# Routing of an expert layer moved four tiles at a time into the end of the attention before it

## The chip, the cores and the metric

One core of a Trainium2 chip. The metric is the device time of one execution in microseconds (us). A core has TensorE (PE, with its weight loads shown as PEld), VectorE (DVE), ScalarE (ACT), GpSimd (POOL) and SyncE (SP), each with its own queue that is worked off in order; they meet only at semaphores. Transfers are issued by SP, ACT and POOL and run on 16 shared DMA engines.

## The reference

A decoder layer on x of 8 x 256 tokens with 256 features, in float32, in three residual parts:

```python
x = x + fast_weight_attention(layernorm(x), W_qkvb, W_o, ln_g, ln_b)
x = x + cross_attention(layernorm(x), context, Wq, Wk, Wv, Wout, bout)   # 8 heads of 128
x = x + experts(layernorm(x), router_w, w1, w2)                          # 8 experts, 1024 hidden

def experts(x):
    probs = softmax(x @ router_w)              # [2048, 8]
    idx = argmax(probs); gate = probs[idx]
    pos = running count of earlier tokens of the same expert
    keep = pos < 256
    expert_in[idx, pos] = x                    # 8 experts x 256 places
    y = (gelu(expert_in @ w1) @ w2)[idx, pos] * gate * keep
```

## The kernel before

Tokens lie in 16 tiles of 128 (HALVES = 2 halves of the 256 rows times T = 8 steps). Tile s * 8 + t holds half s of step t. FLAT lists the tiles in the order of the tokens (t = 0: halves 0 and 1, then t = 1, ...), which is the order in which the router must count.

Three blocks run one after another, each ended by a barrier of all engines: `fast_weight_block`, `cross_block`, `expert_block`.

`cross_block` projects queries, keys and values, then runs one loop over SLOTS = 128 query tiles (8 heads x 16 tiles). In step s of each engine's loop: TensorE computes the scores of tile s (`scores`, L1254), ScalarE the exponential (L1382), VectorE the maxima (L1120, L1122) and a 32x32 transpose (L1135). Since only 32x32 blocks are turned there, 16 moves by DMA (`move`, L939, half issued by SP, half by ACT) finish each transposition for one fourth of the keys of a group of four tiles. LAG = 7 steps behind the scores the moved blocks are split into a high part (ACT, L1376) and a low part (POOL, L1045, and on the last units DVE, L1168), and TensorE adds the weighted values (`weighted`, L1271). Every four units, ACT copies the sum out (`copy_oT`, L1401), TensorE multiplies by the output weights in two halves (`out_project`, L1283), and VectorE scales and adds it to `hall` (`add_output`, L1152). In the last head VectorE then takes the statistics of the two tiles (`row_stats`, L1159 and L1161). After step 127 there are no more scores: steps 128 to 137 are the drain, with only the last weighted sums and outputs. A head's tiles are taken in the order of their number, so the first eight are half 0 of all steps.

`expert_block` begins after the barrier with the routing of all tiles: DVE and ACT normalise the rows (L1625 to L1631), ACT copies the residual rows (L1735), then four "quads" of four tiles in FLAT order go through `row_transposes` (L1791), `copy_zt`, `row_logits` (L1800), `choose` (L1660 to L1673, maximum, one-hot, running counts), `positions` (L1807, L1808) and `place` (L1681 to L1690, slot numbers as int32). POOL scatters each tile's rows into `expert_in` in DRAM by an indirect DMA (L1595), in order, and behind the 16 scatters splits off the low parts of w1 of two experts (L1579). ACT makes the high parts (L1749, L1753), DVE the low part of w2 (L1622). When all scatters have landed, SP loads expert 0's rows (L1550), TensorE transposes them (L1823) and multiplies (L1834, L1846). Eight experts follow each other in a pipeline of two buffers.

```python
            for n, m in enumerate(FLAT):
                if n % 4 == 0:
                    pool.wait_ge(slot_ready, n // 4 + 1)
                pool.indirect_dma_start(xe, ..., z[:, m], None, ...).then_inc(scattered, 16)
            split_low(0, 0)
            split_low(1, 1)
            pool.wait_ge(scattered, 16 * TILES)
```

Of the kernel before, what the change touches and what calls it, by code (L numbers as in the profile page):

```python
# [34 lines left out]
HI, LO = 0, 1  # L35

# [37 lines left out]
WST, CTX = 0, 4 * 4 * 1024  # L74


def fast_weight_block(nc, x, w_qkvb, w_o, context, w_k, w_v, wst, cnat, ident, hall, stats, xe, dots_d, wts_d, beta_d):
# [13 lines left out]
    with ExitStack() as ctx:  # L91
# [12 lines left out]
        for name, span in (("wv", 4 * 2 * DC * NH * DH), ("dots", 4 * 2 * HALVES * T * 2 * HN * CELL),  # L104
                           ("wtok", 4 * TILES * NH * T), ("wqk", 4 * 2 * DC * NH * 2 * DH),
                           ("F", 4 * 2 * BLKS * (2 * BLK + 2)), ("hT", 4 * 2 * DC * TOK), ("ebuf", 4 * 2 * 2 * CHUNK),
                           ("DR", 4 * HG * BLKS * HN * CELL), ("tmp", 4 * 2 * 7 * GCOL)):
            at[name] = start + size
            size += (span + 31) // 32 * 32
# [21 lines left out]
        wo = sb("fw_wo", [P, INNER // P, D])  # L131
# [612 lines left out]
def cross_block(nc, x, ln_g, ln_b, bout, w_q, w_out, wst, cnat, ident, hall, stats, qd, kd, vd):  # L744
# [13 lines left out]
    with ExitStack() as ctx:  # L758
# [9 lines left out]
        for name, span in (("kT0", 4 * 2 * TOK), ("moved", 4 * 3 * TOK), ("kT1", 4 * 2 * TOK), ("pT", 4 * 4 * TOK),  # L768
# [20 lines left out]
        mx = sb("xa_mx", [P, 2])  # L789
        nb = sb("xa_nb", [P, 2])  # L790
        rs = stats
        rinv = sb("xa_rinv", [P, TILES])
        bn = sb("xa_bn", [P, 6])

        OUTS = 5
# [24 lines left out]
        PJ = len(pj)  # L820

# [30 lines left out]
        rows_ln = sem("xa_ln")  # L852

# [30 lines left out]
        def among(s):  # L884
# [3 lines left out]
            return range(EARLY + sum(AMONG[:s]), EARLY + sum(AMONG[:s + 1]))  # L888

# [67 lines left out]
        def _(sp):  # L957
# [31 lines left out]
            for p in range(SLOTS):  # L989
# [10 lines left out]
                for d in (0, 1):  # L1000
                    for a in (0, 2, 1, 3):
                        move(sp, p, a, a ^ d)

        @block.gpsimd
        def _(pool):
# [44 lines left out]
            for s in range(SLOTS):  # L1050
# [4 lines left out]
                for c in chunks_of(s):  # L1055
                    chunk_low(c)

        @block.vector
        def _(dve):
# [79 lines left out]
            def add_output(g, k):  # L1139
# [11 lines left out]
                for m in range(2):  # L1151
                    last = dve.scalar_tensor_tensor(hall[:, i + m], Y[k][:, m], rinv[:, i + m:i + m + 1],  # L1152
                                                    hall[:, i + m], ALU.mult, ALU.add)
                last.then_inc(y_used, 1)

            def row_stats(g, k):
                dve.wait_ge(y_used, 2 * g + k + 1)
                for m in (g % 4 * GT + 2 * k, g % 4 * GT + 2 * k + 1):
                    dve.bn_stats(bn[:], hall[:, m]).then_inc(rows_ln, 1)  # L1159
# [11 lines left out]
            for s in range(SLOTS + LAG + 3):  # L1171
# [5 lines left out]
                if p >= GT and p % GT < 2:  # L1177
# [6 lines left out]
                elif s - LAG + 1 < SLOTS:  # L1184
                    for r in (0, 1):
                        low_part(2 * (s - LAG + 1) + r)

        @block.tensor
        def _(pe):
            def transposes(n):  # L1190
                if n == CTX_BANKS:
                    pe.wait_ge(z_ready[0], 1)
                if n == CTX_BANKS + Z_BANKS // 4:
                    pe.wait_ge(z_ready[1], 1)
                if n >= 4:
                    pe.wait_ge(tp_lo, n - 3)
                for k in range(4):
# [3 lines left out]
                    else:  # L1201
                        c, m = (n - CTX_BANKS) // (TILES // 4), (n - CTX_BANKS) % (TILES // 4) * 4 + k
                        src = z[:, m, c * P:(c + 1) * P]
# [82 lines left out]
            for s in range(SLOTS + LAG + 2):  # L1286
# [7 lines left out]
                if p >= GT and p % GT < 2:  # L1294
                    out_project(p // GT - 1, p % GT)

        @block.scalar
        def _(act):
# [104 lines left out]

            for n in range(Q0, Q0 + 8):
                copy_out(n)
# [7 lines left out]
            for s in range(SLOTS + LAG + 1):  # L1413
                p = s - LAG
                if p >= GT and p % GT == 0:
# [23 lines left out]
def expert_block(nc, r_w, w1, w2, out, ident, hall, stats, xe):  # L1439

    with ExitStack() as ctx:
# [10 lines left out]
        FLAT = [s * T + t for t in range(T) for s in range(HALVES)]  # L1454
        QUADS = TILES // 4
        z = sb("ex_z", [P, TILES, ROW])
        rw = sb("ex_rw", [P, DC, E])
        lg = sb("ex_lg", [P, TILES, E])
        ex = sb("ex_ex", [P, TILES, E])
        oh = sb("ex_oh", [P, TILES, E])  # L1460
        pre = sb("ex_pre", [P, TILES, E])
        rank = sb("ex_rank", [P, E])
        mx = sb("ex_mx", [P, TILES])
        top = sb("ex_top", [P, TILES])
        gate = sb("ex_gate", [P, TILES])
        token = sb("ex_token", [P, TILES], I32)
        pos = sb("ex_pos", [P, TILES])
        slot = sb("ex_slot", [P, TILES])
        sloti = sb("ex_sloti", [P, TILES], I32)
# [425 lines left out]
```

## Time and profile before

| | us |
|---|---|
| median of 3 runs | 1476.18 (1470.36 to 1476.22) |
| profiled execution | 1479.12 |
| its span | 1477.3 |

| engine | busy us | share of the span |
|---|---|---|
| PE | 1344.4 | 91% |
| PEld | 1102.6 | 75% |
| DVE | 1132.8 | 77% |
| ACT | 935.0 | 63% |
| POOL | 867.6 | 59% |

The profile is of one execution. Times in it are counted from the start of the span. A row of the timeline is: start, duration, engine, line of the kernel, operation, output<-inputs, shapes, number of instructions merged into the row, and in brackets the idle time before it with what ended it. "ACTq" and "SPq" are DMA issues by those queues. TensorE's granted clock is given as a share of 2.4 GHz: 1.00 is 2.4 GHz, 0.50 is 1.2 GHz. A busy TensorE is not one at its peak, since the ends of its matmuls are modelled.

### The profile page before, as it was taken

The numbers are of one execution on the slowest core, as the hardware profiler recorded it, in microseconds if no ns is written. First come the engines' busy times: TensorE is split into PE (matmuls) and PEld (weight loads), VectorE is DVE, ScalarE is ACT, GpSimd is POOL, SyncE is SP. The second block draws the span as 40 slices with busy tenths as digits, with TensorE's granted clock in tenths as the row PEclk, the third lists the DMA queues.
The fourth block names the chain that finished last, engine by engine and source line by source line (L and its number), as shares of the span: only waits on it lengthen the run. The fifth ranks groups of instructions, "written<-read, shape, count | busy, mean of one in ns | idle before, by whom it ended". The sixth has DMA issues, their size and how long they took to land. (4 is left out here: it accounts for less than half of the span.)

```text
span 1477.3 us, 22028 instructions
## 1 busy us (share of the span) xinstructions
PE 1344.4 (91%) x7240; PEld 1102.6 (75%) x7240; DVE 1132.8 (77%) x1726; ACT 935.0 (63%) x1278; POOL 867.6 (59%) x525
## 2 busy tenths in 40 slices
PE   3999999998999799999999999999999999765897
PEld 2788888887788577777777777777777777545897
DVE  6789998958415687888888898989898888864454
ACT  3443434116556687778878878888788778532684
POOL 1300012106401598889989989999899879304453
PEclk9999999999999899999999999999999999975899
DMA  9102023206564776777777767777777667636572
GB/s 270 18 7 65 1 65 87 73 14 229 189 221 156 209 210 185 201 187 200 214 180 206 203 188 207 204 199 211 188 204 207 178 173 194 167 97 217 179 252 82
DMA packets 196445, 241.40 MB, mean 163 GB/s; under 512 B 58499, under 2 KB 101893, under 8 KB 196336
## 3 DMA queue, kind: packets, MB, share of 16 engines
q1 hardware_dynamic: 132032, 143.13, 33.9%
q10 hardware_dynamic: 62256, 91.04, 22.5%
q0 software_dynamic: 2048, 5.90, 1.0%
q8 instruction: 54, 0.88, 0.3%
q14 instruction: 55, 0.45, 0.1%
HBM read 64.79 MB, written 41.32 MB: 72 GB/s over the span
## 5 line engine op out<-in xcount | busy, mean ns | idle before, releaser
L1045 POOL TENSOR_TENSOR xa_pT<-xa_moved,xa_pT 128x1024 fp32r<-128x1024 f32 x244 | 581.1, 2404 | 51.7 <-ACT xa_pT L1376 50.6
L1254 PE MATMUL xa_S<-xa_kT,xa_qT 128*128 128x512 f32 x1536 | 399.3, 409 | 40.2 <-ACT xa_probs L1382 38.5
L1254 PEld LDWEIGHTS xa_S<-xa_kT,xa_qT 128*128 128x128 f32 x1536 | 287.6, 192 | 134.3 <-ACT xa_probs L1382 69.9
L1271 PE MATMUL xa_O<-xa_pT,xa_v 128*128 128x512 f32 x1536 | 376.1, 394 | 9.2 <-DVE xa_pT L1168 5.7
L1135 DVE STREAM_TRANSPOSE xa_tq<-xa_probs 128x1024 f32<-128x1024 f32 x256 | 316.9, 1238 | 40.3 <-ACT xa_probs L1382 38.5
L1271 PEld LDWEIGHTS xa_O<-xa_pT,xa_v 128*128 128x128 f32 x1536 | 291.5, 190 | 73.2 <-DVE xa_pT L1168 7.4
L1382 ACT ACTIVATE xa_probs<-xa_S,xa_nb 128x1024 f32<-128x1024 f32 x256 | 286.1, 1118 | 75.6 <-DVE xa_nb L1125 50.1
L1376 ACT ACTIVATE xa_pT<-xa_moved 128x1024 fp32r<-128x1024 f32 x256 | 269.7, 1060 | 86.5 <-issue 69.5
L1120 DVE TENSOR_REDUCE xa_mx<-xa_S 128x1 f32<-128x1024 f32 x128 | 155.8, 1217 | 77.1 <-PE xa_S L1254 76.3
L1122 DVE TENSOR_REDUCE xa_mxp<-xa_S 128x1 f32<-128x1024 f32 x128 | 157.6, 1231 | 18.7 <-PE xa_S L1254 13.6
L461 PE MATMUL fw_pp<-fw_hT,fw_wqk 128*128 128x512 f32 x384 | 99.1, 408 | 9.9 <-DVE fw_F L607 8.3
L330 POOL COPY fw_DR<-fw_tmp 128x6 f32<-128x6 f32 (+1 forms) x80 | 15.8, 199 | 142.5 <-DVE fw_tmp L622 142.5
L461 PEld LDWEIGHTS fw_pp<-fw_hT,fw_wqk 128*128 128x128 f32 x384 | 71.3, 192 | 27.2 <-issue 7.5
L382 ACT ACTIVATE fw_ebuf<-fw_pp 128x1024 f32<-128x1024 f32 x32 | 32.8, 1024 | 82.3 <-PE fw_pp L461 80.4
L626 DVE TENSOR_REDUCE fw_DR<-fw_tmp 128x48 f32<-128x384 f32 (+1 forms) x80 | 71.1, 930 | 0.0
L1040 POOL TENSOR_TENSOR xa_qT<-xa_chunk,xa_qT 128x512 fp32r<-128x512 f32 x31 | 40.3, 1300 | 50.3 <-ACT xa_qT L1366 50.0
L490 PEld LDWEIGHTS fw_gr<-fw_F 64*128 64x128 f32 x1024 | 59.9, 188 | 11.6 <-issue 11.6
L1283 PE MATMUL xa_Y<-xa_wout,xa_oT 128*128 128x256 f32 x256 | 65.7, 379 | 0.7 <-ACT xa_oT L1401 0.7
L490 PE MATMUL fw_gr<-fw_F 64*128 64x65 f32 x1024 | 64.4, 276 | 0.0
L1152 DVE SCALAR_TENSOR_TENSOR hall<-xa_Y,xa_rinv,hall 128x256 f32<-128x256 f32 x128 | 56.1, 480 | 10.4 <-PE xa_Y L1283 8.2
L622 DVE TENSOR_TENSOR fw_tmp<-fw_gr,fw_gmask 128x390 f32<-128x390 f32 (+1 forms) x80 | 43.4, 585 | 26.0 <-PE fw_gr L490 26.0
L284 POOL TENSOR_TENSOR fw_spread<-fw_m,fw_wtok 128x1024 f32<-128x1024 f32 x8 | 18.7, 2345 | 73.3 <-DMA fw_wtok<-fw_wts_d 40.7
(218 smaller groups left out, 1794.6 us busy)
## 6 DMA issues: line engine op xcount, KB each, us to landing
xa_moved<-xa_tq ACTq DMA_DIRECT2D x1024, 64.0 KB, 2.1
xa_moved<-xa_tq SPq DMA_DIRECT2D x1024, 64.0 KB, 2.1
heads_k<-ci_outs SPq DMA_DIRECT2D x32, 256.0 KB, 2.0
heads_v<-ci_outs SPq DMA_DIRECT2D x32, 256.0 KB, 2.2
heads_q<-ci_outs SPq DMA_DIRECT2D x32, 256.0 KB, 2.3
xa_chunk<-heads_v ACTq DMA_DIRECT2D x32, 256.0 KB, 3.1
ex_w1s<-in_L_ffn_w_dram SPq DMA_DIRECT2D x8, 1024.0 KB, 6.9
ex_w2s<-in_L_ffn_w_dram SPq DMA_DIRECT2D x8, 1024.0 KB, 9.0
```

Source lines behind the costliest of these rows:

```text
L461: last = pe.matmul(pp[:, m % 2, kind], wqk[a][:, kind, c, 2 * hp:2 * hp + 2], hT[b][:, c, cols], start=(n == 0), stop=(n == len(parts) - 1))
L490: last = pe.matmul(gr[:, r, g % 2, (k - a) * GCOL:(k - a + 1) * GCOL], F_[d, hp % 2, k, 0:2 * BLK], F_[d, hp % 2, k, BLK:BLK + GCOL], star ...
L626: dve.reduce_sum(DR[:, hg, a:b, h + r, 0:T], tmp[:, r, 0:b - a, 0:BLK].rearrange("p k (b t) -> p k t b", t=T), AX).then_inc(reduced, 1)
L1045: pool.tensor_tensor(quadrants(pT[LO], r), unit_moved(r), quadrants(pT[HI], r).bitcast(F32), ALU.subtract).then_inc(lo_ready, 1)
L1120: dve.reduce_max(mx[:, s % 2:s % 2 + 1], S[:, 0:2].rearrange("p a b -> p (a b)"), AX).then_inc(mx_ready, 1)
L1122: dve.reduce_max(mxp[:, s % 2:s % 2 + 1], S[:, 2:4].rearrange("p a b -> p (a b)"), AX) \
L1135: dve.transpose(tq[:, g % 2, :, u * JT // 2:(u + 1) * JT // 2, m].rearrange("p b j n -> p j b n"), probs[:, unit % RING].rearrange("p (j b ...
L1254: last = pe.matmul(S[:, k], qT[a][:, i // GT % 2, q], kT[b][h % 2][:, k * 512:(k + 1) * 512], start=(n == 0), stop=(n == 2))
L1271: last = pe.matmul(O[:], v[a][:, j * P:(j + 1) * P], pT[b][:, r % PRING, k], start=(j == 0 and n == 0), stop=(j == JT - 1 and n == 2))
L1283: last = pe.matmul(Y[k][:, m], oT[:, t * P:(t + 1) * P], woh[:], start=True, stop=True)
L1376: act.activation(quadrants(pT[HI], r), unit_moved(r), ACT.Copy).then_inc(hi_ready, 1)
L1382: act.activation(probs[:, unit % RING], S[:, 2 * u:2 * u + 2].rearrange("p a b -> p (a b)"), ACT.Exp, bias=nb[:, s % 2:s % 2 + 1], scale=S ...
```

## The change

The routing leaves `expert_block` and becomes part of the loop of `cross_block`, which now has END = 142 steps.

- In the attention a head's tiles are taken in FLAT order, so that each group of four tiles of the last head is one quad of the router. `FLAT[...]` appears where `hall` and the normalised rows are read or written.
- Quad q is routed from step FINAL[q] on, FINAL = 128, 129, 133, 137: root, residual copy and normalising in step FINAL[q], transposes one step later, logits (and the copies in front of them) two, choice and positions three, slots four steps later. The steps of the routing stand behind the work of the attention in each engine's step; TensorE takes the logits of a quad in front of the transposes of the next.
- POOL scatters quads 0 to 2, splits off the low parts of expert 0's w1 and w2, then scatters quad 3. ACT makes the high parts of them in step 135. Before, DVE made w2's low part. Expert 1's w1 is split after the barrier as before in the next block.
- SP loads the router's weights and w1 and w2 of experts 0 and 1 behind the last move, and writes `hall` to the output four tiles at a time.
- ACT changes its function table in advance with instructions on an unused tile (`table`).
- TensorE's transposes of the attention's own normalised rows wait for both halves at once. The arenas in SBUF are laid out anew; some small tiles share places.
- The barrier at the end of `cross_block` now comes after all scatters and output writes. `expert_block` begins with the loads of rows.

The core of the diff:

```diff
+FLAT = [s * T + t for t in range(T) for s in range(HALVES)]
...
+        FINAL = [SLOTS, SLOTS + 1, SLOTS + 5, SLOTS + 9]
+        END = FINAL[-1] + 5
...
+        def due(s, lag):
+            return [q for q, first in enumerate(FINAL) if first + lag == s]
...
 sync:
+            sp.wait_ge(tr_done, 2 * SLOTS)
+            sp.dma_start(rw[:], r_w.rearrange("(c p) e -> p c e", p=P)).then_inc(rw_in, 16)
+            for q in range(GT):
+                sp.wait_ge(arrived[-1][q], MOVES * 7)
+            for i in range(2):
+                sp.dma_start(w1s[i][:], w1[i].rearrange("(c p) f -> p c f", p=P)).then_inc(w_in[i], 16)
+                sp.dma_start(w2s[i][:], w2[i].rearrange("(c p) d -> p c d", p=P)).then_inc(w_in[i], 16)
+            for q in range(QUADS):
+                finished(sp, q)
+                for s in range(HALVES):
+                    sp.dma_start(out...[s, :, 2 * q:2 * q + 2],
+                                 hall[:, s * T + 2 * q:s * T + 2 * q + 2]).then_inc(x1_out, 16)
...
 gpsimd:
+            def scatter(q):
+                pool.wait_ge(slot_ready, q + 1)
+                pool.wait_ge(x1_copied, q + 1)
+                for m in FLAT[4 * q:4 * q + 4]:
+                    pool.indirect_dma_start(xe, bass.IndirectOffsetOnAxis(sloti[:, m:m + 1], 0), rows[:, m], None,
+                                            bounds_check=E * CAP - 1, oob_is_err=False).then_inc(scattered, 16)
...
+            for q in range(QUADS - 1):
+                scatter(q)
+            for n, (split, staged_w) in enumerate(((w1p, w1s), (w2p, w2s))):
+                pool.wait_ge(e_hi, n + 1)
+                pool.tensor_tensor(split[0][LO][:], staged_w[0][:], split[0][HI][:].bitcast(F32),
+                                   ALU.subtract).then_inc(e_lo, 1)
+            scatter(QUADS - 1)
+            pool.wait_ge(scattered, 16 * TILES)
...
 vector:
-                    last = dve.scalar_tensor_tensor(hall[:, i + m], Y[k][:, m], rinv[:, i + m:i + m + 1],
-                                                    hall[:, i + m], ALU.mult, ALU.add)
+                    last = dve.scalar_tensor_tensor(hall[:, FLAT[i + m]], Y[k][:, m], rinv[:, i + m:i + m + 1],
+                                                    hall[:, FLAT[i + m]], ALU.mult, ALU.add)
...
+            def normalise_rows(q):
+                tiles = slice(4 * q, 4 * q + 4)
+                dve.wait_ge(rows_ln, 2 * (4 * q + 4))
+                dve.tensor_scalar(rve[:, tiles], rs[:, tiles, 1], EPS, None, ALU.add).then_inc(rve_ready, 1)
+                dve.wait_ge(rsd_ready, q + 1)
+                then(dve.reciprocal(rrstd[:, tiles], rrstd[:, tiles]))
+                newton_rsqrt(dve, rve[:, tiles], rrstd[:, tiles], rtmp[:, tiles], rt, rt_count[0])
...
-            for s in range(SLOTS + LAG + 3):
+            for s in range(END):
...
+                for q in due(s, 0):
+                    normalise_rows(q)
+                for q in due(s, 2):
+                    copy_zt(q)
+                for q in due(s, 3):
+                    choose(q)
+                for q in due(s, 4):
+                    place_rows(q)
...
 tensor:
                 if n == CTX_BANKS:
-                    pe.wait_ge(z_ready[0], 1)
-                if n == CTX_BANKS + Z_BANKS // 4:
-                    pe.wait_ge(z_ready[1], 1)
+                    for half in z_ready:
+                        pe.wait_ge(half, 1)
...
+            def row_transposes(q):
+                pe.wait_ge(rows_ready, q + 1)
+                if q == 0:
+                    pe.wait_ge(exp_done, 2 * SLOTS)
+                else:
+                    for c in range(DC):
+                        pe.wait_ge(zt_ready[c], q)
+                for c in range(DC):
+                    for k in range(4):
+                        last = pe.transpose(S[:, c, k * P:(k + 1) * P], rows[:, FLAT[4 * q + k], c * P:(c + 1) * P], ident[:])
+                    last.then_inc(ztp, 1)
...
+                for q in due(s, 2):
+                    row_logits(q)
+                for q in due(s, 1):
+                    row_transposes(q)
+                for q in due(s, 3):
+                    positions(q)
...
 scalar:
+            def row_root(q):
+                tiles = slice(4 * q, 4 * q + 4)
+                act.wait_ge(rve_ready, q + 1)
+                act.activation(rrstd[:, tiles], rve[:, tiles], ACT.Sqrt).then_inc(rsd_ready, 1)
+
+            def copy_x1(q):
+                finished(act, q)
+                act.activation(four(rows[:, :, X1:X1 + D], q), four(hall[:], q), ACT.Copy).then_inc(x1_copied, 1)
...
+                for q in due(s, 0):
+                    row_root(q)
+                    copy_x1(q)
+                for q in due(s, 2):
+                    copy_zt(q)
+                for q in due(s, 3):
+                    row_exp(q)
+                    if q == 2:
+                        table(0, ACT.Sqrt)
+                    if q == 3:
+                        table(2, ACT.Gelu_apprx_tanh)
+                if s == FINAL[-1]:
+                    table(1, ACT.Exp)
+                if s == FINAL[-1] - 2:
+                    expert_high(w1p, w1s)
+                    expert_high(w2p, w2s)
```

## Rows read from the trace of the kernel before

**Rows 1.** Windows: stretch, length, busy of PE, PEld, DVE, ACT, POOL; clock, DMA

```profile
1280.00:1311.00 31.00, 21.99 (x72) 16.48 (x73) 21.71 (x39) 10.85 (x11) 0.00 (x0) 0.83 0.50 126
1321.50:1371.60 50.10, 24.33 (x112) 23.69 (x112) 24.54 (x108) 15.00 (x15) 23.33 (x29) 0.50 0.65 221
```

**Rows 2.** Timeline of the drain, 1280 to 1322, ScalarE, TensorE and VectorE

```profile
1282.74 1.06 ACT L1376 ACTIVATE xa_pT<-xa_moved 128x1024 fp32r<-128x1024 f32 x1 [2.87 <-issue]
...
1288.85 1.06 ACT L1376 ACTIVATE xa_pT<-xa_moved 128x1024 fp32r<-128x1024 f32 x1 [3.42 <-issue]
...
1290.15 3.80 ACTq L939 DMA_DIRECT2D xa_moved<-xa_tq  x6
...
1300.92 3.10 PE L1271 MATMUL xa_O<-xa_pT,xa_v 128*128 128x512 f32 x12
1301.38 0.88 DVE L1152 SCALAR_TENSOR_TENSOR hall<-xa_Y,xa_rinv,hall 128x256 f32<-128x256 f32 x2 [3.05 <-PE xa_Y L1283]
...
1303.87 1.02 PE L1283 MATMUL xa_Y<-xa_wout,xa_oT 128*128 128x256 f32 x4
...
1308.59 2.36 DVE L1168 TENSOR_TENSOR xa_pT<-xa_moved,xa_pT 128x1024 fp32r<-128x1024 f32 x2
...
1309.86 4.61 PE L1271 MATMUL xa_O<-xa_pT,xa_v 128*128 128x512 f32 x12 [1.90 <-DVE xa_pT L1168]
...
1321.11 0.18 DVE L1161 BATCH_NORM_AGGREGATE stats<-xa_bn 128x2 f32<-128x6 f32 x1
```

**Rows 3.** Timeline of the routing, 1321.8 to 1352

```profile
1321.80 1.28 ACT L1734 ACT_TABLE_LOAD   x1 [6.69 <-PEq L758]
...
1323.09 0.22 ACT L1734 ACTIVATE ex_rstd<-ex_ve 128x16 f32<-128x16 f32 x1
1323.22 3.61 ACT L1735 ACTIVATE ex_z<-hall 128x4096 f32<-128x4096 f32 x1
...
1324.47 5.26 DVE L1631 TENSOR_SCALAR ex_z<-hall,stats,ex_rstd 128x256 f32<-128x256 f32 x16
...
1339.76 1.95 PE L1791 MATMUL ex_H<-ident,ex_z 128*128 128x128 f32 x8
...
1341.46 0.19 DVE L1681 TENSOR_REDUCE ex_gate<-ex_ex 128x4 f32<-128x32 f32 x1
1341.50 3.42 PE L1800 MATMUL ex_Y<-ex_rw,ex_w2s 128*128 128x8 f32 x16
...
1342.86 0.17 DVE L1690 CAST ex_sloti<-ex_slot 128x4 int32<-128x4 f32 x1
...
1349.23 0.19 DVE L1660 COPY ex_lg<-ex_Y 128x32 f32<-128x32 f32 x1
...
1351.55 0.63 PE L1807 MATMUL ex_Y<-ex_oh,ex_before 128*128 128x32 f32 x2 [1.47 <-DVEq L1673]
```

**Rows 4.** Timeline from the first scatter to the first expert

```profile
1344.07 1.18 POOL L1595 DMA_INDIRECT expert_in<-ex_z,ex_sloti  x1 [21.33 <-issue]
...
1355.56 2.29 DVE L1622 TENSOR_TENSOR ex_w2p<-ex_w2s,ex_w2p 128x2048 fp32r<-128x2048 f32 x1 [0.72 <-ACT ex_w2p L1753]
1356.29 2.40 POOL L1595 DMA_INDIRECT expert_in<-ex_z,ex_sloti  x1 [0.30 <-issue]
...
1365.40 0.98 POOL L1595 DMA_INDIRECT expert_in<-ex_z,ex_sloti  x1 [0.30 <-issue]
1366.39 8.99 POOL L1579 TENSOR_TENSOR ex_w1p<-ex_w1s,ex_w1p 128x2048 fp32r<-128x2048 f32 x2
1367.95 0.89 SPq L1550 DMA_DIRECT2D ex_xn<-expert_in  x2
...
1371.62 1.11 PE L1823 MATMUL ex_tp<-ident,ex_xn 128*128 128x128 f32 x4 [19.00 <-DMA ex_xn<-expert_in]
```

**Rows 5.** All instructions on the normalised rows ci_z: first and last start

```profile
L1204 PE MATMUL xa_S<-ident,ci_z x32: 270/272/276, 406.6 to 426.2; 128*128 128x128 f32 x32
...
L1335 ACT ACTIVATE ci_z<-hall,ci_shift,ci_rstd x8: 585/587/592, 387.2 to 390.7; 128x256 f32<-128x256 f32 x8
```

More of the change, by code:

```diff
@@ L767, in cross_block @@
         size = 0
-        for name, span in (("kT0", 4 * 2 * TOK), ("moved", 4 * 3 * TOK), ("kT1", 4 * 2 * TOK), ("pT", 4 * 4 * TOK),
+        for name, span in (("kT1", 4 * 2 * TOK), ("kT0", 4 * 2 * TOK), ("pad", PAD), ("moved", 4 * 3 * TOK), ("pT", 4 * 4 * TOK),
                            ("tq", 4 * 8 * TOK), ("v", 4 * 2 * TOK), ("probs", 4 * TOK), ("qT", 4 * 2 * 2 * GCOLS)):
@@ L1169, in low_part, with then, wide @@
                                   ALU.subtract).then_inc(lo_ready, 1)
-            for s in range(SLOTS + LAG + 3):
+            rt_count = [0]
+            def then(instruction):
+                instruction.then_inc(rt, 1)
+                rt_count[0] += 1
+                dve.wait_ge(rt, rt_count[0])
+            def wide(a):
+                return a.unsqueeze(3).to_broadcast([P, HALVES, 2, E])
+            def normalise_rows(q):
[5 more added lines that the diff above has]
+                newton_rsqrt(dve, rve[:, tiles], rrstd[:, tiles], rtmp[:, tiles], rt, rt_count[0])
+                rt_count[0] += 4
+                for i in range(4 * q, 4 * q + 4):
+                    last = dve.tensor_scalar(rows[:, FLAT[i], 0:D], hall[:, FLAT[i]], rs[:, i, 0:1], rrstd[:, i:i + 1],
+                                             ALU.subtract, ALU.mult)
+                last.then_inc(rows_ready, 1)
+                dve.wait_ge(consts, 4)
+                dve.tensor_copy(four(rows[:, :, TOKEN], q), four(token[:], q))
@@ L1176, in _ @@
                 p = s - LAG - 1
[L1177 removed]
+                if p >= GT and p % GT < 2 and p < SLOTS + 2:
                     g, k = p // GT - 1, p % GT
@@ L1284, in out_project, with row_logits, positions @@
                 last.then_inc(y_mm, 1)
-            for s in range(SLOTS + LAG + 2):
+            def row_transposes(q):
+                pe.wait_ge(rows_ready, q + 1)
+                if q == 0:
+                    pe.wait_ge(exp_done, 2 * SLOTS)
+                else:
+                    for c in range(DC):
[4 more added lines that the diff above has]
+                    last.then_inc(ztp, 1)
+            def row_logits(q):
+                if q == 0:
+                    pe.wait_ge(rw_in, 16)
+                if q == QUADS - 1:
+                    pe.wait_ge(slot_ready, 1)
+                for c in range(DC):
+                    pe.wait_ge(zt_ready[c], q + 1)
+                for k in range(4):
+                    for c in range(DC):
+                        last = pe.matmul(rp[q][:, k % 2, k // 2], zt[:, (2 * q + c) % 4, k], rw[:, c],
+                                         start=(c == 0), stop=(c == DC - 1))
+                last.then_inc(logits, 1)
+            def positions(q):
+                if q == 0:
+                    pe.wait_ge(consts, 2)
+                pe.wait_ge(oh_ready, q + 1)
+                pe.matmul(rp[q], before[:], four(oh[:], q), start=True, stop=False)
+                pe.matmul(rp[q], ones[:], four(pre[:], q), start=False, stop=True).then_inc(pos_mm, 1)
+            for s in range(END):
                 p = s - LAG
```

333 lines of the change are left out of this document (136 added, 197 removed).

## The prediction

> **What bounds the kernel now.** I read the page's slices first. TensorE is near full in nearly all of them and falls only near the end, where its granted clock falls too. So I asked for busy time by stretch. The fast-weight part and the attention up to about 1275 us are full, and the change puts nothing into them. What it can reach is the stretch from 1280 to 1371.6: the last weighted sums (to 1311), the last outputs (to 1321.3), and then 50 us in which TensorE is busy 24.3 us at a granted clock of 0.50 [rows 1]. After that come 1477.3 - 1371.6 = 105.7 us of experts.
>
> The timeline by instruction gives the order inside it. ScalarE starts the high part of one unit, issues the moves of a later one, and starts the next high part 6.1 us later: its own DMA issues, which end at 1290.15 + 3.80 = 1293.95, set that pace [rows 2]. The last low part ends at 1308.59 + 2.36 = 1310.95, the last weighted sum at 1309.86 + 4.61 = 1314.5, the last row statistics at 1321.3 [rows 2]. The next block begins 0.5 us later and routes all sixteen tiles in one chain [rows 3]. GpSimd stands idle 21.3 us of it until the first slots exist, then issues 16 scatters one behind another, the last at 1365.40. The rows come back to TensorE at 1371.62 [rows 4]. So a stretch of 50.3 us from the last statistics to the first expert is what could be given back. It can only be given back by what is not itself slowed before 1321.
>
> **Parts that cost nothing.** Tiles of a head in router order: the same reads and writes with other indices. TensorE's transposes of the normalised rows now wait for both halves at once. The second half is complete at 390.7 + 0.6 = 391.3 and the first such transpose starts at 406.6, so 15 us of projections hide it; without that cover it would cost the 391.3 - 387.2 = 4.1 us that the second half takes [rows 5]. The arena is laid out in another order with the same overlaps, no work. The loads of two experts' weights go behind SyncE's last move, where its queue has nothing else until the block ends, and GpSimd's constants go in front of its first scatter, where it waits anyway (21.3 us now [rows 4]). ScalarE's two copies of the first expert's weights stand where it otherwise waits for the third quad's logits. If the weights came late, those copies would hold ScalarE's next exponential, and with it the slots of quad 2.
>
> **What is put among the last weighted sums.** The engines' queues are in order, so I follow them. Loop steps are those of the source (128 is the first without scores).
>
> ScalarE reaches the new root of quad 0 at 1282.7, where the high part of step 129 starts now. It loads a table (1.28), takes the root (0.22), copies the residual rows (3.61 for 16 tiles, so 0.9 for four), and starts that high part at 1285.1 [rows 2, 3]. VectorE gets the root at 1284.2 and normalises four tiles: 2.5, from 1323.09 + 0.22 to 1324.47, plus a quarter of 5.26. That is 1286.7. Then 0.35 for two steps as small as the last of the statistics (0.18), 2.25 for output and statistics (0.88 for the addition at 1301.38, the rest for two tiles' statistics), and 2.36 for two low parts: 1291.7. Only behind these stands the variance of quad 1 (0.2, as other steps of its size), and ScalarE waits for it with the moves of a later unit behind it. Root and copy 1.1: the high part that began at 1288.85 begins at 1293.0 [rows 2, 3]. This is the new wait that I think costs most.
>
> Its issues take the 5.1 us that they take now, to 1298.1, and the copy of the transposed rows 0.5 by the rate of the residual copy. TensorE, in front of the weighted sum of unit 124, waits for that copy, does the logits of quad 0 (3.4) and the transposes of quad 1 (1.95): 1304.0 [rows 2, 3]. From there it is TensorE's own work that counts. A weighted sum took 3.1 at the higher and 4.6 at the lower clock [rows 2]. I take 4.6 for unit 124 and the middle, 3.85, for 125 to 127. So: 1304.0 + 4.6 + output product 1.0 + logits 3.4 + positions 1.2 + 3.85 + 1.0 + 1.2 + 3.85 + 3.85 = 1328.0 (positions are two groups of 0.6). VectorE's part up to its last low part comes to about 1324, just in time. The last weighted sum thus ends 13.5 us later than 1314.5.
>
> The last outputs. Transposes of quad 2 1.95, output product 1.0, logits of quad 2 3.4 stand in front of the second output product: 1334.3. VectorE chooses for quad 2 (2.3, from 1349.23 to 1351.55) and only then adds the last two tiles (0.35 + 2.25): 1339.2, against 1321.3 now [rows 2, 3].
>
> **The tail.** Quad 3 is normalised in 2.9, and behind it VectorE places quad 2 (1341.46 to 1343.03, 1.6): 1343.7. GpSimd's first scatter of quad 2 follows 1.0 later (as 1344.07 follows 1343.03), four take 4 x 1.28 = 5.1 (0.98 and a gap of 0.30 each), to 1349.8 [rows 3, 4]. Next in its queue are two low parts of weights, 9.0: 1358.8. Then the last four: the fourth starts 0.3 + 3.84 later, at 1363.0. Landing and passing on 2.55 (1365.40 to 1367.95), the block's end 0.5 (1321.3 to 1321.8), load until TensorE reads it 3.67: 1369.8 [rows 2 to 4]. Quad 3's slots would be ready by 1343.7 + 0.5 + 3.4 + 2.3 + 1.2 + 1.6 = 1352.7, so the two low parts hold the last scatters by some 5 us. They cost nothing where they were, since the first expert waited for its rows.
>
> **Sum.** From the last statistics to the first expert 1369.8 - 1339.2 = 30.6 us instead of 50.3, a gain of 19.7; the last statistics 17.9 later; left 1.8 us. The experts (105.7) are the same. The profiled execution took 1479.12 for its span of 1477.3; the median of the runs is 1476.18, 2.9 lower. 1476.2 - 1.8 = 1474.4.
>
> **Bounds of what no row shows.** TensorE's clock among mixed work: at 3.1 (2.4 GHz) for all of 125 to 127 the sum gains 2.3 more, at 4.6 it loses 2.3. Logits and transposes at the higher clock would take about half, some 8 us less in all before 1334; in the routing of now the granted clock stays at 0.50, the lower level of 1.2 GHz, though TensorE is half busy with just these [rows 1, 3], so I take the slow ones. Whether ScalarE's table load stands ahead of a wait: it started at 1321.80 with the block, so ahead; behind it, 1 to 3 us more. The delay before the last weighted sum can't well be under 4: VectorE gets 13.0 us of new work before its last low part (two quads normalised 5.8, copies 1.0, choices 4.6, one placed 1.6) and was idle 31.0 - 21.7 = 9.3, TensorE gets two each of logits, transposes, positions, 13.1, and was idle 31.0 - 22.0 = 9.0 [rows 1, 3].
>
> The table load of the trace is 1.28 [rows 3]. The Trainium skill (ScalarE: Activation LUTs, section What ACT_TABLE_LOAD costs) gives the same 1.28 and adds a drain of 1.38 for every change of set; its section Table sets: the hidden batching unit asks to batch functions by set, which this change does not: root and exponential alternate. Here the root started at 1323.09, right behind the load, with no drain visible behind it. By the Trainium skill's figure the one exposed load would be 1.4 dearer, and the time 1475.8.
>
> **Rivals.**
> (A, the forecast) 1474.4, chance 0.48.
> (B) The pieces fill waits instead of lengthening chains. The delay before the last weighted sum is then the 4.1 of the bound instead of 13.5: 1474.4 - 9.4 = 1465.0. For it: the idle 9 us on each engine, and waits such as TensorE's 1.9 before the last weighted sum [rows 1, 2]. Against: the queues are in order and logits stand in front of weighted sums. Chance 0.28.
> (C) No gain that shows: the weighted sums stay at 4.6 or more and the table loads fall behind waits: 2.3 + 2 us on A, 1478.7, the routing moved and the time with it. Chance 0.14.
> (D) Slower: a scatter's issue took 2.40 once instead of 0.98, when VectorE ran a 2.29 us subtraction at 1355.56 [rows 4]. If all eight scatters of the last two quads take that, 8 x 1.42 = 11.4 on A: 1485.8. It decides from seven of them on. Against it: the first and the last took 1.18 and 0.98, the first beside small VectorE work, which is all that there is then. Chance 0.10. The Trainium skill (GPSIMD Engine Reference, Key points) says that GpSimd shares its SBUF interfaces with VectorE and contends with instructions with two SBUF inputs; the one slow scatter agrees.
>
> **Numbers.** About 0.5% (7.4 us, 1468.8 to 1483.6) is what a measurement of this kernel can tell from no change. Faster 0.30 (B and a little of A), same 0.60, slower 0.10. Range 1463 to 1484: B with some of TensorE's work at the higher clock below, C with loads behind waits above.
>
> **What the profile after would show.** The last weighted sum ends near 1328 (B: under 1320). ScalarE waits for the variance of quad 1 some 3 us at 1289 to 1292. TensorE waits in front of logits 0 until about 1298.6. Last statistics near 1339. The GpSimd queue goes scatter, two low parts of 4.5, last scatters near 1359 to 1363, with slots ready 5 us before. First expert at about 1370, and 105.7 us behind it. It is wrong if the drain is delayed under 8 us, if the last scatters go out before 1355, or if the experts' stretch changes.

## The result, and the profile after

| | us |
|---|---|
| changed kernel, median of 10 runs | 1481.08 (1477.75 to 1493.77) |
| kernel before, median of 10 runs | 1473.70 (1470.36 to 1476.22) |
| ratio | 1.0063, 95% interval 1.0037 to 1.0088 |
| profiled execution after | 1481.31, span 1479.6 |

The change made the kernel slower: by 7.4 us between the medians (0.50%), by 0.63% in the ratio of the runs, whose interval is clear of 1. The forecast was 1474.4, 1.8 us of gain, most likely no difference that can be told. The time lies inside the range, but slower had a chance of only 0.10, and by a mechanism that is not the one that acted.

Windows of the changed kernel: first the time until the last weighted sum, then from the last statistics to the first expert, then the experts. The columns are those of [rows 1].

```profile
1280.00:1329.00 49.00, 34.13 (x137) 27.10 (x138) 34.09 (x104) 19.05 (x24) 5.16 (x4) 0.76 0.72 213
1338.50:1374.80 36.30, 6.58 (x28) 5.98 (x28) 16.93 (x42) 6.87 (x9) 18.66 (x11) 0.50 0.23 84
1374.80:1479.60 104.80, 96.44 (x800) 95.83 (x800) 51.32 (x79) 66.14 (x93) 46.23 (x23) 0.96 0.52 172
```

The first row answers to the first of [rows 1]: the drain now reaches to 1329 and holds more work of every engine. The second is what is left of the routing, 36.3 us instead of 50, but VectorE's 16.9 us in it is odd: most of the quads are routed already. The timeline tells what it is. First the drain, which answers to [rows 2]:

```profile
1270.19 1.22 DVE L1216 TENSOR_REDUCE xa_mx<-xa_S 128x1 f32<-128x1024 f32 x1 [0.47 <-PE xa_S L1421]
...
1290.64 0.21 ACT L1612 ACTIVATE ex_rstd<-ex_ve 128x4 f32<-128x4 f32 x1 [4.70 <-DVE ex_ve L1280]
...
1295.94 0.60 ACT L1622 ACTIVATE ex_zt<-xa_S 128x512 f32<-128x512 f32 x1 [2.24 <-issue]
...
1300.89 0.62 SPq L1060 DMA_DIRECT2D ex_rw<-in_L_ffn_router_w_dram  x1
...
1302.95 3.58 PE L1474 MATMUL xa_S<-ex_rw,ex_zt 128*128 128x8 f32 x16 [8.02 <-DMA ex_rw<-in_L_ffn_router_w_dram]
...
1312.21 1.85 PE L1474 MATMUL xa_S<-ex_rw,ex_zt 128*128 128x8 f32 x16
...
1314.36 3.02 PE L1438 MATMUL xa_O<-xa_pT,xa_v 128*128 128x512 f32 x12
...
1324.80 4.37 PE L1438 MATMUL xa_O<-xa_pT,xa_v 128*128 128x512 f32 x12 [1.98 <-DVE xa_pT L1264]
...
1338.36 0.18 DVE L1257 BATCH_NORM_AGGREGATE stats<-xa_bn 128x2 f32<-128x6 f32 x1
```

Read the bracket of the first logits (1302.95): TensorE sat idle 8.02 us until a DMA brought the router's weights. SyncE had issued that load at 1300.89, behind all its moves; ScalarE's copy of the transposed rows had been ready since 1295.94 + 0.60 = 1296.5. The first row is the last tile's first maximum, used as a mark below.

Then the tail, which answers to [rows 3, 4]:

```profile
1342.86 0.17 DVE L1329 CAST ex_sloti<-ex_slot 128x4 int32<-128x4 f32 x1
...
1347.67 0.98 POOL L1133 DMA_INDIRECT expert_in<-ex_z,ex_sloti  x1 [0.30 <-issue]
1347.87 0.19 DVE L1301 COPY ex_lg<-xa_S 128x32 f32<-128x32 f32 x1 [4.24 <-PE xa_S L1474]
1348.10 0.19 DVE L1302 TENSOR_REDUCE ex_mx<-ex_lg 128x4 f32<-128x32 f32 x1
1348.32 9.36 DVE L1303 TENSOR_TENSOR ex_ex<-ex_lg,ex_mx 128x32 f32<-128x32 f32 x1
1348.66 4.52 POOL L1149 TENSOR_TENSOR ex_w1p<-ex_w1s,ex_w1p 128x2048 fp32r<-128x2048 f32 x1
1353.12 4.51 POOL L1149 TENSOR_TENSOR ex_w2p<-ex_w2s,ex_w2p 128x2048 fp32r<-128x2048 f32 x1
1357.61 0.18 DVE L1304 TENSOR_TENSOR ex_oh<-ex_lg,ex_mx 128x32 f32<-128x32 f32 x1
...
1361.59 0.17 DVE L1329 CAST ex_sloti<-ex_slot 128x4 int32<-128x4 f32 x1
1362.56 0.99 POOL L1133 DMA_INDIRECT expert_in<-ex_z,ex_sloti  x1 [4.93 <-DVE ex_sloti L1329]
...
1366.41 0.97 POOL L1133 DMA_INDIRECT expert_in<-ex_z,ex_sloti  x1 [0.30 <-issue]
...
1371.02 0.90 SPq L1749 DMA_DIRECT2D ex_xn<-expert_in  x2
...
1374.81 1.11 PE L1873 MATMUL ex_tp<-ident,ex_xn 128*128 128x128 f32 x4 [14.38 <-DMA ex_xn<-expert_in]
```

The row to stop at is L1303: a subtraction of 128x32 elements that "took" 9.36 us. Its twin one line later takes 0.18. It ends when GpSimd's second low part ends (1353.12 + 4.51 = 1357.63, and 1348.32 + 9.36 = 1357.68). By the rows it began 0.34 us before GpSimd's first low part; rows on GpSimd are rough, so these starts don't tell which came first. That the two low parts held it is a reading so far; e1, e2 and e4 below test it. So the busy time of VectorE in the window above is mostly one instruction that was held.

**A common mark.** The start of the last maximum before the drain differs by up to 6.5 us between executions (1265.4 to 1271.9), without a change in front of it that would explain it: 3.8 of them lie between two executions of the changed kernel (changed and c1). So I cut each trace at four points: that mark, the end of the last statistics, the first expert (the transposes of its rows on TensorE), the end of the span. The runs of this table are described below.

| kernel | mark | to last statistics | on to first expert | on to the end | sum |
|---|---|---|---|---|---|
| before | 1271.17 | 50.1 | 50.3 | 105.7 | 206.1 |
| order of tiles alone (o1) | 1265.37 | 48.0 | 50.4 | 105.2 | 203.5 |
| changed | 1270.19 | 68.4 | 36.3 | 104.8 | 209.4 |
| changed, again (c1) | 1266.41 | 68.8 | 36.2 | 105.1 | 210.1 |
| low parts on VectorE (e1) | 1267.02 | 68.7 | 29.4 | 104.7 | 202.7 |
| router's weights early (e2) | 1266.47 | 62.3 | 36.3 | 105.2 | 203.7 |
| both (e3) | 1266.13 | 60.8 | 29.3 | 104.9 | 195.0 |
| both, again (c2) | 1265.83 | 60.7 | 29.2 | 104.9 | 194.9 |
| low parts in pieces (e4) | 1270.96 | 68.8 | 33.4 | 104.5 | 206.7 |
| GpSimd's low parts earlier (s1) | 1271.92 | 71.7 | 27.1 | 105.2 | 204.0 |
| low parts in gaps (e6) | 1271.03 | 62.5 | 27.1 | 104.9 | 194.5 |
| low parts in gaps, again (c3) | 1267.51 | 62.3 | 27.1 | 104.6 | 194.1 |
| routing after the drain (l1) | 1269.95 | 50.4 | 57.7 | 104.7 | 212.9 |

Each column is a difference of starts and ends in that kernel's timeline (changed: 1338.54 - 1270.19 = 68.4, 1374.81 - 1338.54 = 36.3, 1479.6 - 1374.81 = 104.8). The stretches repeat within 0.5 us between two executions of one kernel (changed and c1, e3 and c2, e6 and c3), much better than whole times do. The exception is the kernel before: its profiled execution had the last weighted sum at 4.61 us [rows 2], o1's took 3.06, and its own 1479.12 is 5.4 over its median of ten. Against o1 the change costs 5.9 to 6.6 us in this table, against the profile of before 3.3; the medians say 7.4. So the table places costs by stretch; for whole times the medians and ratios count, and the two can differ by some 2 to 4 us (e3 against o1 is 8.6 in the table, e3 against before 4.7 by its medians).

### The profile page after: what moved, and what is told of

It is laid out like the page before. It is cut to its first block and busy times, and to the rows that moved or that the text cites. A ratio compares the mean times of both kernels' runs of the same rounds, so it can differ in the third digit from the quotient of the medians.

```text
span 1479.6 us, 22085 instructions
## 1 busy us (share of the span) xinstructions
PE 1341.2 (91%) x7240; PEld 1093.3 (74%) x7240; DVE 1142.6 (77%) x1746; ACT 939.3 (63%) x1289; POOL 871.9 (59%) x526
## 5 line engine op out<-in xcount | busy, mean ns | idle before, releaser
L1438 PE MATMUL xa_O<-xa_pT,xa_v 128*128 128x512 f32 x1536 | 380.0, 397 | 6.7 <-DVE xa_pT L1264 6.6
L1421 PEld LDWEIGHTS xa_S<-xa_kT,xa_qT 128*128 128x128 f32 x1536 | 284.6, 190 | 131.0 <-ACT xa_probs L1587 67.3
```

What stands on the lines that cost most here:

```text
L1421: last = pe.matmul(S[:, k], qT[a][:, i // GT % 2, q], kT[b][h % 2][:, k * 512:(k + 1) * 512], start=(n == 0), stop=(n == 2))
L1438: last = pe.matmul(O[:], v[a][:, j * P:(j + 1) * P], pT[b][:, r % PRING, k], start=(j == 0 and n == 0), stop=(j == JT - 1 and n == 2))
```

## The experiments

The two theories at the start: T1, GpSimd's two low parts held VectorE, and the cost is there; T2, the drain delayed by the late router's weights sets the time. In the expectations of later runs the names T1 and T2 stand for what is said there.

**e1, low parts on VectorE.** The two subtractions go from GpSimd's queue to the end of VectorE's, behind its last slots:

```diff
-            for n, (split, staged_w) in enumerate(((w1p, w1s), (w2p, w2s))):
-                pool.wait_ge(e_hi, n + 1)
-                pool.tensor_tensor(split[0][LO][:], staged_w[0][:], ...)
             scatter(QUADS - 1)
...
+            for n, (split, staged_w) in enumerate(((w1p, w1s), (w2p, w2s))):
+                dve.wait_ge(e_hi, n + 1)
+                dve.tensor_tensor(split[0][LO][:], staged_w[0][:], ...)
```

> The changed kernel with one edit: the two low parts of the first expert's weights go from GpSimd (between the third and the fourth quad's scatters) to VectorE, behind its last slots. Theory 1 (they hold the tail twice: GpSimd's scatters behind them, and VectorE's subtraction in the choice of quad 3, which stood 9.36 us beside them at 1348.32): slots of quad 3 at about 1352.5 instead of 1361.8, last scatter near 1357, first expert near 1365.5 instead of 1374.8, and 9 us less than the changed kernel: about 1472. Theory 2 (only GpSimd's queue order counts, VectorE's long row is an artefact of the record): the choice would still take over 5 us somewhere, slots of quad 3 stay near 1361, and the gain is under 3 us: about 1478 to 1481.

1472.27 against 1470.53 for before on that chip, ratio 1.0013 (1.0001 to 1.0024). The changed kernel has 1.0063, and 1.0051 when run again (c1), so the edit is worth 0.38% to 0.50%, 5.6 to 7.4 us. That is T1, less than its 9 us; its 1472 was met because before is 3.2 faster on this chip. T2 had under 3 us. Its timeline, the same choice and the scatters behind it:

```profile
1345.46 0.19 DVE L1299 TENSOR_TENSOR ex_ex<-ex_lg,ex_mx 128x32 f32<-128x32 f32 x1
1345.57 0.18 DVE L1300 TENSOR_TENSOR ex_oh<-ex_lg,ex_mx 128x32 f32<-128x32 f32 x1
...
1349.56 0.17 DVE L1325 CAST ex_sloti<-ex_slot 128x4 int32<-128x4 f32 x1
1349.63 2.29 DVE L1353 TENSOR_TENSOR ex_w1p<-ex_w1s,ex_w1p 128x2048 fp32r<-128x2048 f32 x1
1350.52 2.24 POOL L1133 DMA_INDIRECT expert_in<-ex_z,ex_sloti  x1 [4.75 <-DVE ex_sloti L1325]
1351.83 2.29 DVE L1353 TENSOR_TENSOR ex_w2p<-ex_w2s,ex_w2p 128x2048 fp32r<-128x2048 f32 x1
1353.07 1.90 POOL L1133 DMA_INDIRECT expert_in<-ex_z,ex_sloti  x1 [0.30 <-issue]
1355.28 0.97 POOL L1133 DMA_INDIRECT expert_in<-ex_z,ex_sloti  x1 [0.30 <-issue]
```

The held step is 0.19 again, and the tail is 6.9 us shorter (36.3 to 29.4). The price shows too: two scatters take 2.24 and 1.90 instead of 0.97 beside VectorE's subtractions, 2.2 us together. (Slots 9.2 us sooner behind the last statistics, less 2.2, is the 6.9.)

**e2, router's weights early.** Their tile gets a place of its own, so the load needs no free arena and goes in front of the moves:

```diff
-        rw = home("ex_rw", "probs", [P, DC, E], F32, 4 * (7 * P + 3 * TILES))
+        rw = sb("ex_rw", [P, DC, E])
...
+            sp.dma_start(rw[:], r_w.rearrange("(c p) e -> p c e", p=P)).then_inc(rw_in, 16)
...
             sp.wait_ge(tr_done, 2 * SLOTS)
-            sp.dma_start(rw[:], r_w.rearrange("(c p) e -> p c e", p=P)).then_inc(rw_in, 16)
```

> The changed kernel with one edit: the router's weights are loaded into a small tile of their own in front of all moves instead of behind the last one. Theory 1 (the logits of quad 0 stood 8.0 us for this load, issued at 1300.89 at the end of SyncE's queue, and TensorE's order then held the weighted sums behind them): the logits start near 1297 instead of 1303, the last weighted sum ends about 5 us earlier (1324), and the first expert starts 4 to 6 us earlier: about 1476. Theory 2 (the drain is bounded by ScalarE's and VectorE's work and the clock would be lower when the logits come earlier, so the wait was hidden): last weighted sum within 2 us of 1329, total within 2 us of the changed kernel's.

1472.72 against 1470.53, ratio 1.0023 (1.0008 to 1.0038). By the ratios that is 5.9 us under the changed kernel (4.1 against c1's), as theory 1 has it; theory 2 had it within 2. The drain is 6.1 to 6.5 us shorter (62.3), the tail the same 36.3, and VectorE's step is held as before:

```profile
1292.22 0.60 ACT L1621 ACTIVATE ex_zt<-xa_S 128x512 f32<-128x512 f32 x1 [2.24 <-issue]
...
1292.96 3.26 PE L1473 MATMUL xa_S<-ex_rw,ex_zt 128*128 128x8 f32 x16 [2.30 <-ACT ex_zt L1621]
...
1338.54 9.34 DVE L1302 TENSOR_TENSOR ex_ex<-ex_lg,ex_mx 128x32 f32<-128x32 f32 x1
```

The logits now wait 2.30 us for ScalarE's copy, as the prediction had it, and start 0.14 behind its end.

**e3, both edits.**

> Both edits of the two runs before together. If the two waits stand one behind the other on the chain to the first expert, the gains add: 9 + 5 us, about 1467, which is below the kernel before (1474). If one hides the other, the time is that of the better of the two alone.

1465.83 against 1470.53, ratio 0.9978 (0.9964 to 0.9991): faster than before. The two gains add, one in the drain and one in the tail: 0.50% and 0.40% alone, 0.85% together (12.5 us, 14 forecast). So neither T1 nor T2 alone; each names about half.

**e4, the low parts in pieces.** They stay on GpSimd in the same place, each cut in eight instructions of 256 columns.

```diff
+                for k in range(8):
+                    c = slice(k * TOK // 8, (k + 1) * TOK // 8)
+                    pool.tensor_tensor(lo[:, c], st[:, c], hi[:, c].bitcast(F32), ALU.subtract).then_inc(e_lo, 1)
```

> The changed kernel with GpSimd's two low parts of 2048 columns cut into eight pieces of 256 each, in the same place. Theory 1a (VectorE can't start while one GpSimd instruction holds the shared path, and gets in between two): the step of 9.36 us shortens to one or two pieces, 0.6 to 1.3 us, and each of the next VectorE steps with two inputs from SBUF waits for about one piece too. Theory 1b (VectorE gets in only when GpSimd's queue has nothing ready): the long step stays at 9 us or over. Theory 2 (an artefact): the row shortens to 0.19 and nothing else in the tail moves.

One run, 1479.43, which tells nothing by its time; its rows do. VectorE beside the pieces:

```profile
1349.32 0.19 DVE L1304 TENSOR_REDUCE ex_mx<-ex_lg 128x4 f32<-128x32 f32 x1
1349.55 0.47 DVE L1305 TENSOR_TENSOR ex_ex<-ex_lg,ex_mx 128x32 f32<-128x32 f32 x1
1349.87 5.48 POOL L1152 TENSOR_TENSOR ex_w1p<-ex_w1s,ex_w1p 128x256 fp32r<-128x256 f32 x8
1349.94 0.75 DVE L1306 TENSOR_TENSOR ex_oh<-ex_lg,ex_mx 128x32 f32<-128x32 f32 x1
...
1350.72 0.64 DVE L1307 TENSOR_TENSOR ex_oh<-ex_oh,ex_rank 128x32 f32<-128x32 f32 x1
1351.40 0.18 DVE L1309 TENSOR_REDUCE ex_top<-ex_oh 128x4 f32<-128x32 f32 x1
1351.62 0.42 DVE L1310 TENSOR_TENSOR ex_oh<-ex_oh,ex_top 128x32 f32<-128x32 f32 x1
1352.08 2.66 DVE L1315 TENSOR_TENSOR ex_pre<-ex_pre,ex_oh 128x8 f32<-128x8 f32 x4
...
1355.32 5.47 POOL L1152 TENSOR_TENSOR ex_w2p<-ex_w2s,ex_w2p 128x256 fp32r<-128x256 f32 x8
1355.95 0.19 DVE L1325 TENSOR_TENSOR ex_lg<-xa_S,ex_oh 128x32 f32<-128x32 f32 x1 [0.65 <-PE xa_S L1485]
1356.18 0.18 DVE L1326 TENSOR_REDUCE ex_pos<-ex_lg 128x4 f32<-128x32 f32 x1
...
1356.69 0.77 DVE L1328 TENSOR_SCALAR ex_top<-ex_top 128x4 f32<-128x4 f32 x1
1357.50 0.64 DVE L1329 TENSOR_TENSOR ex_slot<-ex_slot,ex_pos 128x4 f32<-128x4 f32 x1
```

The held step shrinks from 9.36 to 0.47, and the next ones are held in turn, as theory 1a has it. Theory 1b (9 us or over) falls, and theory 2 too, since the steps behind it and the tail moved. No step is held for 9 us any more; each that is held takes 0.4 to 0.8, about one piece (5.48 / 8 = 0.69). And not every step is held: the reductions (0.18) and the product that reads one operand from PSUM (`xa_S`, 0.19) run beside the same pieces unhindered, those with two operands in SBUF and a small step with one (L1328) are held. The tail is 2.9 us shorter (33.4), and GpSimd pays 1 us more for each low part. The Trainium skill (GPSIMD Engine Reference, Key points) says that GpSimd shares SBUF interfaces with VectorE and contends with instructions in a two-port mode or with two SBUF inputs. The reductions and the PSUM operand agree with it; whether L1328 ran in a two-port mode no row shows. The Trainium skill (SBUF — State Buffer, section SBUF: two separate sides) calls it an exclusive lock for the whole instruction of whoever starts first; by that and the rows here the step would be held for one low part, an estimate of 4.5 us. The measured step was held through two back to back, 9.36. Theory 1a would have one, too: it fits the pieces but not the whole low parts, and that stays open.

**s1, low parts earlier on GpSimd.** e2, and the two low parts in front of the third quad's scatters instead of the last quad's.

> The changed kernel with the early load of the router's weights, and GpSimd's two low parts in front of the third quad's scatters instead of behind them, where its queue is empty for 8 us. Theory 1 (while GpSimd subtracts, VectorE's instructions with two inputs from SBUF, and its copies and scalar steps, can't start): a long VectorE row of 4 to 9 us appears in another place, in the normalising of quad 3 or the output step before it, and the time is not better than with the low parts behind the third quad: 1473 or more. Theory 2 (only what stands in front of the last scatters in GpSimd's own queue counts): no long row, the last scatters leave 1 us after their slots, and the time is that of the run with both edits: 1466.

1474.56 against 1471.11, ratio 1.0023 (1.0004 to 1.0041), as e2. Its tail is 9.2 us shorter than e2's, 27.1, but the hold has moved into the drain (71.7 instead of 62.3):

```profile
1330.60 10.20 DVE L1313 TENSOR_TENSOR ex_pre<-ex_pre,ex_oh 128x8 f32<-128x8 f32 x4
...
1331.61 4.51 POOL L1148 TENSOR_TENSOR ex_w1p<-ex_w1s,ex_w1p 128x2048 fp32r<-128x2048 f32 x1
1336.06 4.50 POOL L1148 TENSOR_TENSOR ex_w2p<-ex_w2s,ex_w2p 128x2048 fp32r<-128x2048 f32 x1
```

Four steps of 0.19 take 10.20, and the last outputs and statistics stand behind them. Theory 1 is right in kind and in the time; the row is longer than its 4 to 9 and stands in the running counts of quad 2, ahead of the place it named. An idle stretch of GpSimd's queue was not free either, since VectorE had steps of the path beside it.

**l1, routing after the drain.** e3, but all four quads behind the last weighted sums:

```diff
-        FINAL = [SLOTS, SLOTS + 1, SLOTS + 5, SLOTS + 9]
+        FINAL = [SLOTS + 9, SLOTS + 10, SLOTS + 11, SLOTS + 12]
...
-                    if q == 2:
-                        table(0, ACT.Sqrt)
```

> The version with both edits, but with all four quads routed behind the last weighted sum (FINAL = 137 to 140 instead of 128, 129, 133, 137). It tells what putting them among the weighted sums is worth. Theory 1 (the mixing lengthens the last weighted sums by 10 us or more but lets 12 of the 16 scatters leave early, which is worth more): the last statistics come as early as in the kernel before, the first slot some 22 us behind them, 16 scatters of 1.28 one behind another, the first expert about 51 us behind the statistics, the total within 3 us of the kernel before, 4 to 7 us over the version with both edits. Theory 2 (the mixing is a loss as such): faster than the version with both edits.

1482.95 against 1471.11, ratio 1.0076 (1.0048 to 1.0103). The drain is back at 50.4, the tail is 57.7. Both sizes expected were off. It is 14.4 us behind e3 by the ratios and 17.9 in the table, so against this order the mixing is a gain, and the view that it is a loss falls. That is not what the mixing is worth against the kernel before, since l1 is itself 12 us worse than before. Its tail has 7.3 of them: the first slots come at 1346.52, 26.3 us after the last statistics, against 21.7 before [rows 2, 3], which I put down to quads one step apart in a loop written for mixing, and the block's end adds 2 (below). The rest is not placed. Against the kernel before, the mixing with both repairs is worth 4.7 to 7.4 us by the medians (e3, c2, e6, c3).

**o1, order of tiles alone**, in the kernel before: `FLAT[...]` in the attention, its transposes waiting for both halves.

> The kernel before with the tiles of a head in the router's order alone, its routing unchanged. All theories: no change, within 0.2% of the kernel before. If it is slower by 3 us or more, part of the loss of the changed kernel lies outside the drain and the routing.

1471.47 against 1471.11, ratio 1.0005 (0.9989 to 1.0022). No cost, as forecast.

**e6, low parts in gaps.** e2, with w1's low part on VectorE while it waits for the last logits, and w2's in the next block while the rows are loaded:

```diff
+                if s == FINAL[-1] + 2:
+                    dve.wait_ge(e_hi, 1)
+                    dve.tensor_tensor(w1p[0][LO][:], w1s[0][:], ...).then_inc(e_lo, 1)
...
-            dve.sem_inc(w2_lo, 1)
+            split_low(0, 0)
```

> The changed kernel with the early load of the router's weights; the low part of w1 on VectorE where it waits for the last logits, that of w2 on VectorE at the start of the expert block, where it waits for the rows. In the run with both edits the two stood beside the last four scatters and stretched two of them from 0.97 to 2.24 and 1.90. Theory 1: the last four scatters take 1.28 each again, 2 us less than with both edits, about 7 us under the kernel before. Theory 2 (the scatter's own DMA bounds the end, not its issue): no change against both edits.

1465.95 against 1471.11, ratio 0.9959 (0.9943 to 0.9974). One scatter beside VectorE's subtraction took 2.84, but of quad 2 and not on the path; the last four took 0.97 each, and the tail is 2.2 us shorter than e3's, as theory 1 has it. The drain is 1.7 longer, near e2's: its first logits took 3.6 (two rows, from 1297.67 to 1301.23) and e2's 3.26, e3's 1.92. In the second executions it is the same, 2.54 in c3 and 1.92 in c2. The granted clock over them goes along: 0.50 in the changed kernel (3.58) and in e6, 0.55 in e2, 0.73 in c3, 1.00 in e3 and c2. So it is the clock that differs there; what lowers it in some of these kernels is not shown. By whole times e6 and e3 can't be told apart.

**c1, c2, c3: changed, e3 and e6 on one chip**, since e3 and e6 had run on different ones.

> The changed kernel itself, beside the two that follow, on one chip. Both theories: 0.3% to 0.9% above the kernel before, 1474 to 1482 us.

> Router's weights early and both low parts on VectorE behind the last slots. If the two costs are the whole of the loss (T1): some 14 us under the changed kernel, about 1466 us. If the last slots' place sets the end alone (T2), this one, whose first expert begins 4.5 us before that of the kernel with the low parts in gaps, is 3 to 5 us faster than it.

> The first expert's low parts on VectorE, one before the last choice, one in the expert block. T2: 3 to 5 us slower than the kernel with both behind the last slots, by its later first expert. T1': equal within 1.5 us, since the later start is made up in the first expert, whose matmuls then wait less for split weights.

| on one chip, before 1470.39 | us | ratio |
|---|---|---|
| changed (c1) | 1477.49 | 1.0051 (1.0033 to 1.0068) |
| both (c2) | 1464.26 | 0.9962 (0.9947 to 0.9977) |
| in gaps (c3) | 1462.95 | 0.9947 (0.9931 to 0.9963) |

The change's cost repeats, and either repair takes 13 to 14.5 us off it. c3 and c2 are not told apart (the intervals overlap), so T2's 3 to 5 us fall. The expectation of a later first expert by 4.5 us came from starts counted from the span's start (1356.18 and 1360.64 in e3 and e6). Counted from the mark it is 90.1 and 89.6: the 4.5 us were the drift in front of it. So T1' has the equality right and its reason wrong: there is no later start to make up, and the stretch from the first expert on is 104.9 and 104.6.

## Why the prediction was wrong

**The step that failed is the sum of the tail**, 30.6 us, measured 36.3. The text priced the two low parts in GpSimd's queue alone ("next in its queue are two low parts of weights, 9.0") and let the slots of quad 3 be ready at 1352.7 beside them. GpSimd's side is right to 1.2 us: they ran from 1348.66 to 1357.63, forecast to 1358.8. But they held VectorE's choice, so the slots came at 1361.76, and the last scatter at 1366.41 instead of 1363.0: 3.4 us. Rival D had the shared interface in hand and asked only what VectorE does to GpSimd's scatters, not what GpSimd does to VectorE. Another 1.6 us is the block's end: from the last scatter to SyncE's load 1371.02 - 1366.41 = 4.61 instead of 3.05. The 0.5 was taken from a barrier that came behind the statistics [rows 2, 3]; here it stands behind landed scatters. From the start of the last scatter to the first expert it took 6.2 and 6.3 in before and o1, and 8.35 to 8.48 in the eleven executions whose block ends between landing and load, whatever else they had: 2.1 us more, of which the forecast had 0.5. So the first expert came 5.0 later than forecast (1374.81 against 1369.8); the tail is 5.7 longer, since the last statistics ended 0.7 sooner.

The list of what the profile after would show has one sign that failed: slots of quad 3 ready 5 us before the last scatters. They came at 1361.76, 0.8 before the first of the four. The three signs named there for being wrong did not come: the drain was delayed by more than 8, the last scatters left behind 1355, the experts took 104.8 instead of 105.7. They tested the parts that held. The chapter on the chip said that the engines meet only at semaphores; the held step shows that GpSimd and VectorE meet without one.

With the low parts gone from GpSimd (e1) the tail is 29.4, 6.9 less. That is more than 3.4 us, since the forecast already had them hold the last scatters by some 5 us.

**The drain's total was right by luck, its terms were not.** From the last maximum to the last statistics the forecast comes to 1339.2 - 1271.2 = 68.0, measured 68.4 and 68.8; the last weighted sum ended at 1329.17, forecast 1328.0. But TensorE began the first logits at 1302.95, not 1298.6, for a wait that no term had: under "Parts that cost nothing" the experts' weights were set behind SyncE's last move, and the router's load in the same place was passed over, although its reader stands in the drain. Against that, from the transposes behind those logits to the last weighted sum it took 20.8 instead of 24.0: the second logits 1.85 instead of 3.4, the weighted sums 3.5, 3.0, 3.0 and 4.4 instead of 16.15 in all. From 1310.20 to 1316.00 the granted clock was 1.00, the upper level. The bounds had both clocks; for the weighted sums the middle was taken, for the logits the lower one. e2 shows what the two errors hid: without the wait the drain takes 62.3, 60.8 in e3.

**Had the hold and the block's end been seen**, the forecast would have been 1479.4, still within what can't be told from no change: the drain as forecast, the tail 5.0 longer, so 1.8 of gain becomes 3.2 of loss, which is what the two profiles show at the first expert (1374.81 against 1371.62). Of the other 4.2 us of the measured 7.4, some 2.6 come from the profile of before: it was a long execution, 5.4 over the median of ten, with a granted clock of 0.86 from the mark to the last statistics, where o1 has 0.93; o1's stretch is 2.1 shorter and its sum 2.6. The forecast subtracted 2.9 for it at the end, but the delay in the drain was worked out from the slow one. The last 1.6 are not placed. The base of the forecast, a median of three, was also 2.5 over that of ten, which moves the time forecast and not the difference.

**Right**: order of tiles (o1), the wait of ScalarE for quad 1's variance as a new wait (4.70 us, forecast some 3), constants, high parts (two of 1.90, with no wait for weights), the slots of quad 2 at 1343.03 (forecast 1343.7), and experts unchanged (104.8 and 105.7). **Rivals**: B (the last weighted sum delayed by 4.1) did not happen. It ended 59.0 behind the mark, against 43.3 before. In e3, without the late load, it ended at 50.1, a delay of 6.8: there B's 4.1 is nearer than A's 13.5. Of C's table loads one followed a wait (at 1308.99, behind ScalarE's 9.46 for the transposes), but the next weighted sums, at 1314.36 and 1319.81, began right behind the positions. D's slow scatter came once, in quad 0 (2.03); the eight of the last two quads took 0.97 to 0.99.

**Open**: why the hold spans two whole low parts rather than one, although VectorE got in between pieces; and the 2.1 us at the block's end, where no experiment took the barrier apart.

## What to carry to other kernels

When an instruction moves on one engine, price it in its neighbours' queues too: on GpSimd, 9 us of subtraction in SBUF also stopped VectorE for 9 us. For every load that moves with its stage, ask who reads it first; a 0.6 us issue at the end of a queue of moves cost 6 to 8 us. With these two repaired, routing among the weighted sums was 4.7 to 7.4 us faster than before instead of 7.4 slower, so look for a misplaced wait before judging the idea; and compare stretches from a common event, since the starts drift by more than the effect.

## What the runs showed of the hardware

A VectorE step of 0.19 us stood 9.34 to 9.36 us beside two GpSimd subtractions of 4.5 back to back, and 0.4 to 0.8 beside pieces of 0.69; reductions and a step with one operand in PSUM were not held beside the pieces. The other way, an indirect DMA's issue of 0.97 took 1.90 to 2.84 beside a VectorE subtraction of 2.29. In the changed kernel the same logits took 3.58 behind 8.02 us of idle TensorE (granted clock 0.50), 1.85 between weighted sums (1.00) and 3.55 in the tail (0.50): being placed among large matmuls halved them only where the clock was up.
